# Deformable convolution on one core: one transfer per batch for positions and one for weights, the latter from GpSimd's queue

## What is computed

```
om = conv3x3(x, w_off) + b_off                    # 27 channels: 9 off_y, 9 off_x, 9 logits
py = off_y + h + ky ; px = off_x + w + kx         # one position per pixel and tap
y0, x0 = floor(py), floor(px)
sampled = bilinear(x, py, px) * sigmoid(logits)   # four neighbours, zero outside the image
out = einsum("bckhw,ock->bohw", sampled, w) + b
out = relu(batchnorm(out)) + x
```

## Time and profile before

| | |
|---|---|
| median of three executions | 2781.42 us |
| the profiled execution | 2780.72 us, span 2778.9 us |
| PE / DVE / ACT / POOL busy | 59% / 56% / 52% / 1% |
| DMA queue q1 (SP) | 136852 packets, 286.47 MB, 53.9% of 16 engines |
| DMA queue q10 (ACT) | 60758 packets, 72.05 MB, 8.3% |
| instruction loads, q8 | 222 packets, 3.64 MB |
| idle before line 945 (DVE), until PE's sampling | 547.2 us |
| idle before line 901 (ACT), until PE's sampling | 457.7 us |

### The profile page before, as it was taken

The page is one execution under the profiler, slowest core; times in us unless marked ns, Lnnn a source line. Parts: engine busy times, 40 slices in busy tenths (PEclk is TensorE's granted clock), DMA queues, the critical chain, the costliest instruction groups (busy, mean ns, idle before and its releaser), DMA issues. The chain is left out here.

```text
span 2778.9 us, 66692 instructions
## 1 busy us (share of the span) xinstructions
PE 1631.9 (59%) x24206; PEld 1106.2 (40%) x24207; DVE 1556.4 (56%) x1718; ACT 1454.1 (52%) x2219; POOL 24.0 (1%) x17
## 2 busy tenths in 40 slices
PE   5559900000058866868668686786776867876340
PEld 5433300000046545545445454554554645554120
DVE  5250055455157756767557575575766756876214
ACT  2112233323058756767557676675766856875001
POOL 1000000000100000000000000000000000000000
PEclk9689955555569988889889898898988988998555
DMA  2377855675877868668676686676866867772006
GB/s 97 83 192 216 221 160 171 185 229 162 199 117 133 133 99 138 114 106 137 98 115 118 109 140 101 103 132 105 140 102 110 137 106 121 133 123 43 3 0 284
DMA packets 197854, 362.34 MB, mean 130 GB/s; under 512 B 87600, under 2 KB 175975, under 8 KB 181737
## 3 DMA queue, kind: packets, MB, share of 16 engines
q1 hardware_dynamic: 136852, 286.47, 53.9%
q10 hardware_dynamic: 60758, 72.05, 8.3%
HBM read 253.93 MB, written 104.46 MB: 129 GB/s over the span
## 5 line engine op out<-in xcount | busy, mean ns | idle before, releaser
L945 DVE TENSOR_TENSOR G<-odd_y,ps_odd_v 128x1008 f32<-128x1008 f32 (+2 forms) x464 | 541.8, 1168 | 547.2 <-PE ps_odd_v L822 547.1
L805 PE MATMUL ps_odd_y<-rows,sel 32*128 32x504 f32 (+1 forms) x896 | 468.2, 523 | 576.3 <-DMA rows<-scratch_parts 417.9
L822 PE MATMUL ps_even_v<-tent_x,stage 32*128 32x171 f32 (+2 forms) x5568 | 592.4, 337 | 238.1 <-issue 220.7
L901 ACT COPY even_v<-ps_even_v 128x1008 f32<-128x1008 f32 (+2 forms) x464 | 450.7, 971 | 457.7 <-PE ps_odd_v L822 456.6
L822 PE MATMUL ps_odd_v<-tent_x,stage 32*128 32x171 f32 (+3 forms) x5568 | 603.7, 331 | 34.6 <-issue 34.5
L895 ACT COPY odd_y<-ps_odd_y 128x504 f32<-128x504 f32 (+2 forms) x928 | 526.3, 567 | 98.5 <-PE ps_odd_y L805 95.7
L822 PEld LDWEIGHTS ps_even_v<-tent_x,stage 32*128 32x128 f32 x5568 | 474.4, 200 | 246.1 <-issue 227.4
L953 DVE TENSOR_TENSOR G<-even_v,ps_even_y 128x1008 f32<-128x1008 f32 (+2 forms) x464 | 538.5, 1161 | 16.8 <-PE ps_even_y L796 14.5
L840 PE MATMUL ps_r<-G,conv_w 128*32 128x224 f32 (+1 forms) x8832 | 515.6, 363 | 5.5 <-issue 4.8
L822 PEld LDWEIGHTS ps_odd_v<-tent_x,stage 32*128 32x128 f32 x5568 | 480.3, 200 | 43.6 <-issue 43.6
L805 PEld LDWEIGHTS ps_odd_y<-rows,sel 32*128 32x128 f32 x896 | 175.6, 196 | 759.4 <-issue 462.1
(11 more groups left out here) (139 smaller groups left out, 897.1 us busy)
## 6 DMA issues: line engine op xcount, KB each, us to landing
place<-scratch_px SPq DMA_DIRECT2D x256, 441.0 KB, 7.0
rows<-scratch_parts SPq DMA_DIRECT2D x256, 220.5 KB, 11.0
scratch_parts<-parts ACTq DMA_DIRECT2D x9, 3136.0 KB, 12.2
scratch_parts<-parts ACTq DMA_DIRECT2D x9, 2688.0 KB, 19.6
x<-scratch_xh SPq DMA_DIRECT2D x48, 406.0 KB, 6.0
scratch_om<-om ACTq DMA_DIRECT2D x64, 196.0 KB, 7.0
scratch_conv<-res SPq DMA_DIRECT2D x448, 14.0 KB, 3.2
image<-scratch_xh SPq DMA_DIRECT2D x4, 1682.0 KB, 25.2
```

The lines of the kernel that those rows point to most:

```text
L805: nc.tensor.matmul(ps_odd_y[:, lo:hi], sel[32 * g:32 * g + 32, :], taps(rows, 32 * g, 32, p, lo, hi), start=True, stop=True).then_inc(odd_ ...
L822: m = nc.tensor.matmul(sub(ps_v[g // 2], 0, 128, i * 512 + lo + first, dims), stage[32 * g:32 * g + 32, j * IMAGE + v * C:j * IMAGE + (v + ...
L901: nc.scalar.copy(two(even_v[p % 3], ROW, 2 * p), two(ps_v[0], 512, 2 * p)).then_inc(even_kept, 1)
L945: nc.vector.tensor_tensor(two(G, ROW, v, slot(v)), two(odd_y[p % 3], ROW, v), two(ps_v[1], 512, v), ALU.mult).then_inc(odd_weighted, 1)
```

## The change

- In DRAM, a batch block now holds, for each image, the even and the odd views of a batch next to each other (`BLOCK_STRIDE`, `KIND_STRIDE`), so the four groups of a pair are four blocks in a row. The groups are now: even view of image 0, odd of image 0, even of image 1, odd of image 1; the matmuls pick their groups accordingly.
- `place` of a batch is one DMA to 128 partitions. Its source is four blocks, each read 32 times.
- `rows` of a batch is one DMA to the 64 even partitions, four blocks of 16 kinds, asked for from GpSimd's queue. `sel` picks even partitions.
- The data of the last, one-step batch is stored in slots of batch 0 that were zero before. So the zero stores and the eight DMAs of the last batch go; GpSimd copies 504 columns of `place` and of `rows` into the small buffers, ordered by writes to a small tile `turn`. The first reload of `place` in a pair waits for the new semaphore `place_read` instead of `distant`.
- In the weights stage the partitions of the tiles hold (quarter, image) instead of (image, quarter), which turns round the outer two counts of the three loads and of the four stores of the ranges. Where a store of seven rows is cut, its last row now goes in two DMAs (96 and 32 partitions) instead of one.
- The 12 DMAs of an image band are issued in another order.

```diff
-PARITY_STRIDE = (4 * B + 1) * BATCH
-KIND_STRIDE = 2 * PARITY_STRIDE
+BLOCK_STRIDE = 2 * B * BATCH
+KIND_STRIDE = 4 * BLOCK_STRIDE
...
-                base = parity * PARITY_STRIDE + tap * GROUP * W
+                base = parity * BATCH + tap * GROUP * W
                 if (q + ky - parity) // 2 == 0:
-                    return [(base, 0, GROUP)]
-                return [(base + W, 0, GROUP - 1), (base + BATCH, GROUP - 1, 1)]
-
-            EDGES = ((0, 0, 3, 6), (0, 4 * B, 0, 3), (1, 0, 6, 3), (1, 4 * B, 0, 6))
+                    return [(base, 0, 128, 0, GROUP)]
+                return [(base + W, 0, 128, 0, GROUP - 1), (base + BLOCK_STRIDE, 0, 96, GROUP - 1, 1),
+                        (base, 96, 32, GROUP - 1, 1)]
...
                     for tile, kind in ((logit[b], 2), (oy[b], 0), (ox[b], 1)):
                         sp.dma_start(tile[:, :], dram("om", (kind * KK + n) * HW,
-                                                      [[OM_IMG, B], [DCH, 4], [1, DCH]])).then_inc(loaded[b], 16)
+                                                      [[DCH, 4], [OM_IMG, B], [1, DCH]])).then_inc(loaded[b], 16)
...
-                        sp.dma_start(dram(name, n * H, [[KK * H, B], [RPC, 4], [1, RPC]]),
+                        sp.dma_start(dram(name, n * H, [[RPC, 4], [KK * H, B], [1, RPC]]),
...
-                        sp.dma_start(sub(tile[BUFFERS[n]], 32 * g, dims[1], 0, [[W, KK], [1, W]] if last else [[1, BATCH]]).bitcast(fp32),
-                                     dram(name, block, [dims] + ([[GROUP * W, KK], [1, W]] if last else [[1, BATCH]]))
-                                     ).then_inc(loaded[BUFFERS[n]], 16)
...
                 def load_place(pair, n):
-                    load("px", place, place_loaded, pair, n, [0, 32])
+                    sp.dma_start(place[n % 2][:, :], dram("px", n * BLOCK_STRIDE + pair * 4 * BATCH,
+                                                          [[BATCH, 4], [0, 32], [1, BATCH]])).then_inc(place_loaded[n % 2], 16)
...
+                def load_rows(pair, n):
+                    pitch = rows[n % 2][:].ap[0][0]
+                    pool.dma_start(bass.AP(tensor=rows[n % 2][:].tensor, offset=0, ap=[[2 * pitch, 64], [1, BATCH]]).bitcast(fp32),
+                                 dram("parts", n * BLOCK_STRIDE + pair * 4 * BATCH,
+                                      [[BATCH, 4], [KIND_STRIDE, Y_KINDS], [1, BATCH]])).then_inc(rows_loaded[n % 2], 16)
...
+                def body(it, last):
+                    wait(pool, distant, STEPS * it)
+                    pool.wait_ge(place_loaded[0], 16 * (2 * it + 1))
+                    pool.tensor_tensor(turn[:, 0:1], turn[:, 4:5], turn[:, 4:5], ALU.add)
+                    pool.tensor_copy(sub(place[2], 0, 128, 0, [[W, KK], [1, W]]),
+                                     sub(place[0], 0, 128, 0, [[GROUP * W, KK], [1, W]])).then_inc(place_loaded[2], 1)
+                    wait(pool, even_spread, STEPS * it)
+                    pool.wait_ge(rows_loaded[0], 16 * (2 * it + 1))
+                    pool.tensor_tensor(turn[:, 1:2], turn[:, 4:5], turn[:, 4:5], ALU.add)
+                    pool.tensor_copy(sub(rows[2], 0, 128, 0, [[W, KK], [1, W]]),
+                                     sub(rows[0], 0, 128, 0, [[GROUP * W, KK], [1, W]]).bitcast(fp32)).then_inc(rows_loaded[2], 1)
+                    pool.wait_ge(distant, STEPS * it + GROUP)
+                    pool.wait_ge(place_loaded[2], it + 1)
+                    pool.tensor_tensor(turn[:, 2:3], turn[:, 4:5], turn[:, 4:5], ALU.add).then_inc(place_read, 1)
+                    pool.wait_ge(rows_loaded[2], it + 1)
+                    for n in range(BATCHES - 1):
+                        if n + 2 < BATCHES - 1 or not last:
+                            pool.wait_ge(even_spread, STEPS * it + GROUP * (n + 1))
+                            load_rows(it + (n + 2) // (BATCHES - 1), (n + 2) % (BATCHES - 1))
```

More of the change, by code:

```diff
@@ L540, in _ @@
                 sp.dma_start(column[:, :], dram("column", 0, [[W, 128], [1, W]])).then_inc(grid_loaded, 16)
[L541 to L545, removed]
                 for n in range(KK):
@@ L589, in store @@
                     for q in range(2):
-                        for to, row, count in runs(n, q):
-                            act.dma_start(dram("parts", to, [[BATCH, 128], [KIND_STRIDE, Y_KINDS], [1, count * W]]),
-                                          sub(parts[b], 0, 128, q * HALF + row * W, [[DCH, Y_KINDS], [1, count * W]]).bitcast(fp32)
+                        for to, part, npart, row, count in runs(n, q):
+                            act.dma_start(dram("parts", to, [[2 * BATCH, npart], [KIND_STRIDE, Y_KINDS], [1, count * W]]),
+                                          sub(parts[b], part, npart, q * HALF + row * W, [[DCH, Y_KINDS], [1, count * W]]).bitcast(fp32)
                                           ).then_inc(stored[b], 16)
@@ L649, in program @@
             G = sb("G", G_SLOTS * 2 * ROW)
+            turn = sb("turn", 5, parts=1)
             res = sb("res", UPX)
@@ L686, in taps, with arrived @@
                 return sub(tile[BUFFERS[n]], part, parts, lo // W * pitch + p % GROUP * W, [[pitch, (hi - lo) // W], [1, W]])
-            def times(n, it):
-                return it + 1 if BUFFERS[n] == 2 else 2 * it + n // 2 + 1
+            def arrived(loaded, n, it):
+                if n == BATCHES - 1:
+                    return loaded[2], it + 1
+                return loaded[n % 2], 16 * (2 * it + n // 2 + 1)
             def slot(v):
@@ L711, in _ @@
             def _(sp):
[L712 to L719 removed]
                 def load_place(pair, n):
[L722 to L725 removed]
+                    sp.dma_start(place[n % 2][:, :], dram("px", n * BLOCK_STRIDE + pair * 4 * BATCH,
+                                                          [[BATCH, 4], [0, 32], [1, BATCH]])).then_inc(place_loaded[n % 2], 16)
                 def load_stage(pair, c):
                     first, count = BANDS[c]
[L729 to L730 removed]
+                    for j, (x0, lo, hi) in enumerate(COLUMNS):
+                        for g in (0, 2, 1, 3):
                             sp.dma_start(sub(stage, 32 * g + lo - x0, hi - lo, j * IMAGE + first * C, [[1, count * C]]),
[L732 removed]
+                                         dram("xt", ((pair * 2 + g // 2) * W + lo) * XT_ROW + (TOP - 5 + first) * C,
                                               [[XT_ROW, hi - lo], [1, count * C]])).then_inc(stage_loaded[c], 16)
@@ L753, in body @@
                             if n + 2 < BATCHES - 1 or not last:
[L754 removed]
+                                if n == 0:
+                                    sp.wait_ge(place_read, it + 1)
+                                else:
+                                    sp.wait_ge(distant, STEPS * it + GROUP * (n + 1))
                                 load_place(it + (n + 2) // (BATCHES - 1), (n + 2) % (BATCHES - 1))
[L756 to L763 removed]
                         for c, (first, count) in enumerate(BANDS):
```

55 lines of the change are left out of this document (19 added, 36 removed).

## The result

| | before | after |
|---|---|---|
| median of the runs, us | 2783.14 (2772.18 to 2787.36, 4 runs) | 3757.94 (3744.26 to 3776.50, 4 runs) |
| ratio to before, 95% interval | | 1.3515 (1.3442 to 1.3588) |
| profiled execution, us (its span) | 2780.72 (2778.9) | 3762.92 (3761.2) |

The change makes the kernel 35% slower. 3190 us were predicted, with a range up to 3690 us: the sign is right, the size is not, and the time is outside the range.

A forecast was written before the change was run, and what follows sets the result against it. The prediction took the sampling stage, with PE stalled behind DMA bursts, as today's bound and four DMA engines as the new one: 2781 + 306 + 85 + 20 = 3192, predicted 3190 us, range 2560 to 3690.

The forecast's parts named there:

- How many engines a DMA gets: All DMAs: the largest number up to 16 dividing both sides' outermost counts; the new `place` gets 4 engines.
- Points 1 to 3: Sampling stage: `place` and other transfers on four engines set a pace of 130 us per pair against 110.9, +306 us.
- point 1: `place` on four engines: 68 to 137 us per pair at 26.7 to 13.2 GB/s each; 106 us taken at 17.
- Point 7: SP's queue: fewer issues; ACT's wait for result stores behind `place` grows inside the pair's pace, adding nothing.
- point 3: Sampling stage: a pair needs 130 us with buffer handover; one `place` takes 26 us and ACT waits; +306 us.
- Point 4: Weights stage: the three loads on four engines lengthen 8 of 9 taps, +85 us taken, +78 to +180 if slowed.
- Point 5: Start of the sampling stage: two `place` loads stand ahead of the first image bands, +20 us (0 to 45).
- Point 6: GpSimd: two copies of 504 columns, 0.4 to 3 us each, at most 6 us per pair, taken as nothing.
- A: Rival: transfers get all 16 engines, PE's branch stall falls to 3 to 5 us; 2540 us (2450 to 2650), chance 0.22.
- B: Rival: four engines at full rate, PE's instructions come by the other twelve; 2650 to 2700 us, chance 0.13.
- C: Rival: GpSimd's queue brings `rows` late, deciding from a landing of 17.3 us; 2845 us, chance 0.05.
- full bound: Upper end of the forecast case with all bounds at their slowest: 167 us per pair, 3900 us in all.

The follow-up runs named there:

- e8_res2: The changed kernel with three buffers for `res`, used in turn, instead of one: 3242 us.
- e10: e4 with each `rows` DMA writing 16 neighbouring partitions instead of the 16 even ones of 32: 2936 us; it does not compute the convolution.
- e4: The changed kernel with `place` as four DMAs of 32 partitions and `rows` as four of 16 even partitions, all on 16 engines: 2751 us.
- e2: The changed kernel with the weights-stage loads `logit`, `oy` and `ox` in four DMAs of 32 partitions each: 3698 us.
- f1: The changed kernel with `place` and weights-stage loads split for 16 engines, and `rows` one DMA per batch with 64 outermost on both sides: 2646 us.
- h1: The kernel before the change with only `rows` moved to the 16 even partitions of each 32, `sel` picking from them: 2632 us.
- e1: The changed kernel with `place` loaded as four DMAs of 32 partitions again, so on 16 engines: 2859 us.
- e3: The changed kernel with the result stores asked for from ACT's queue instead of SP's: 3385 us.

## Why the prediction was right in its sign and wrong in its size

**How many engines a DMA gets** was right, and read from the right place: 4 semaphore packets per `place`, a share of 0.25.

**Points 1 to 3**, the work of the four engines: 17 GB/s and 130 us per pair were taken, +306 us. The after kernel doesn't show this pace. e8_res2 does: once nobody waits for the stores, `place` is the bound and a pair costs 132 us, the stage 2112 - 1783 = +329 us. These points were right to 10%. In the after kernel `place` alone ran at 18 GB/s per engine. The 17 GB/s was a choice between the two bounds, so its closeness is partly luck; that the pace is set by these engines is what e8 bears out.

The bounds of the rate rest on the earlier trace rows. 72 GB/s on four engines and 33 on two, 18 and 16.5 for each, lie between its 13.2 and its 26.7. The Trainium skill's page "SBUF — State Buffer", section "Door 1: The DMA port swizzle", puts partitions 0 to 31 and 32 to 63 behind the same ports, so that two of the four engines can meet there: the slow end of point 1. The rates between the bounds leave open how far they do; one engine by itself was not measured. For `rows` the trace agrees with the page: by its formula 16 neighbouring partitions reach 4 ports and the 16 even ones of 32 reach 8, and a packet takes 1.8 us in e10 and 1.0 in e4.

**Point 7 is the step that failed**: "That wait will grow, inside the pace of point 3". It named the right wait and put it in the wrong place. A wait lies inside the pace of a bound resource only if that resource goes on working through it. Here it doesn't: `place` is only asked for when a buffer is free, a buffer is only freed by steps, and the steps stand behind the store, which stands behind `place`. So the wait comes on top: 516 us of the 982, measured by taking it away (e8), against 0 in the sum. Of the 841 us of the stage, 329 are the pace and 512 this wait.

**Point 4**, the weights stage: +85 taken, +110 measured, inside the range of 78 to 180, but for a second reason beside the first: splitting the loads gives back only 60 us (e2), less than the 78 that the engines were to cost at the least. The other 50 us, some 5 us per tap, had no term, and their cause is open.

**Point 5**, the start: +20 taken, 144 - 110 = +34 measured, inside its range.

**Point 6**, the copies on GpSimd: nothing taken. They take 0.6 us each, and in the list of waits nobody stands behind them.

**The rivals.** A (16 engines, 2540 us) did not happen, but most of its price can be read from f1: `rows` in one DMA with 16 engines on even partitions, and `place` still in four DMAs, makes a stage of 1599 us, 184 of the 240 us that it promised. One `place` DMA to all 128 partitions on 16 engines was not run. The branch stall doesn't fall to 3 to 5 us in any run; the smallest maximum is 8.8 us (e8), and f1's is 10.2. In the section on what bounds the kernel that stall was read as a wait for the engines' burst to end. In h1 `rows` lands 2.7 us earlier and the stall is 3.4 us shorter, so part of the reading holds; but 10.7 us remain, and what sets them was not tried. The 13.7 us that rival A gives this stall stand in no row: the rows have 13.04 and 14.18. B (four engines at full rate) falls with the 72 GB/s. C (GpSimd late) falls with e1: `rows` in 19.8 us, 2.5 us above the point from which C decides, costs PE 13 us in all.

**The range** failed for its upper end: 3690 us were allowed where the text's own full bound was 3900. That bound would have held the 3758 us by luck, with the slowest rate in the place of the wait. The wait of point 7 had no bounds at all; worked out as the rest was, each store that follows a `place` would have waited for up to the 26 us of one `place` (point 3).

**What was missed in the change** was its good part. Rival A gives the partitions of `rows` a few us, and the sum gives them nothing, though the earlier trace rows has the row: 116 GB/s for 16 neighbours, 219 for 32, 436 for 128. By itself this edit is worth 5.3% (h1).

## What to carry to other kernels

Before several DMAs are merged into one, look at the outermost count of both sides: here the merged one got no more engines than that count allowed, and what shared its queue stood behind it on those engines. With 64 outermost on both sides (f1) the merging paid in its stage. When a resource becomes the bound, ask of each wait on it whether the resource has work while it lasts; if the next request needs the waiting engine's progress, add the wait and don't hide it. For a DMA that writes 16 partitions, try them spread out.

## What the runs showed of the hardware that was not expected

- Every second partition instead of 16 neighbours, with the same bytes and packets, took `rows` from 11.2 to 8.7 us (e10, e4), a packet from 1.8 to 1.0 us and the kernel from 2936 to 2751 us. One DMA to all 64 even partitions (f1) took 0.7 us per packet.
- Small stores landed after up to 32.8 us behind `place` on SP's queue, and after at most 17.2 us from ACT's queue (e3).
- A DMA from GpSimd's queue with a source of 4 blocks of 16 makes 272 packets (1088 in four, 64 each with data), one with a single row of 64 blocks 80 (320 in four).
- Two DMAs in a row with outermost count 2 use the same two engines: a share of 0.13, not 0.25.
